# Batch attention in a perceiver kernel: norms inverted ahead of the rotation, spread in ScalarE's banks, and three moves with it

## The reference

```
q = l2norm(xn @ Wq); k = l2norm(xn @ Wk); v = xn @ Wv          # norm over the 32 features of a head
clock = softplus(xn @ clock_w + clock_b)                       # one value per token and head
q, k = rope(q), rope(k)
gcp = exp(clip(cumsum(-softplus(xn @ gate_w + gate_b)), -60, 50))
p_exp = exp(p - max(p)) * clock;  p_cs = cumsum(p_exp)         # p = xn @ p_w + p_b
q = q * gcp / (p_cs + 1e-8);  k = k / (gcp + 1e-8) * p_exp
out = softmax(causal(q k^T / sqrt(32))) @ v;  x1 = out @ out_w + out_b + residual
```

## Time and profile before

| what | value |
|---|---|
| time, median of 3 runs | 2138.5 us (2136.87 to 2139.09) |
| the profiled execution: its own time | 2137.74 us |
| its span | 2136.0 us |
| TensorE busy, granted clock over the span | 2058.3 us (96%), 0.988 |
| VectorE, ScalarE, GpSimd busy | 1230.1, 888.0, 60.9 us |

### The profile page before, as it was taken

One profiled execution on the slowest core, in us unless ns is written; L12 is line 12 of the kernel. 1 busy time (PEld: TensorE's weight loads), 2 busy tenths in 40 slices (PEclk: granted clock), 3 DMA queues, 4 the chain that ended last, 5 costly groups with the idle time before them and its releaser, 6 DMA issues. The chain is left out here.

```text
span 2136.0 us, 35519 instructions
## 1 busy us (share of the span) xinstructions
PE 2058.3 (96%) x14806; PEld 1499.0 (70%) x14806; DVE 1230.1 (58%) x2118; ACT 888.0 (42%) x2081; POOL 60.9 (3%) x78
## 2 busy tenths in 40 slices
PE   7999997999999999989999999999999999989999
PEld 6864454688868888744448887778778777775687
DVE  6446687653438888999996112443443534447563
ACT  4233532442333333689993332322322322333342
POOL 0000000000000000200000000000000000000122
PEclk9999998999999999999999999999999999999999
DMA  6300000112010111200021355211311311233001
GB/s 258 106 21 0 2 2 2 60 60 79 20 46 20 60 60 40 99 20 20 1 79 60 101 138 158 82 54 46 91 46 46 91 46 47 69 120 97 1 0 40
DMA packets 80223, 127.59 MB, mean 60 GB/s; under 512 B 7216, under 2 KB 40496, under 8 KB 79600
## 3 DMA queue, kind: packets, MB, share of 16 engines
q1 hardware_dynamic: 80064, 125.32, 18.5%
HBM read 110.23 MB, written 15.07 MB: 59 GB/s over the span
## 5 line engine op out<-in xcount | busy, mean ns | idle before, releaser
L1272 ACT ACTIVATE R<-bank 128x512 f32<-128x512 f32 (+3 forms) x151 | 89.2, 597 | 407.9 <-PE bank L945 325.5
L1538 ACT ACTIVATE R<-R 128x64 f32<-128x64 f32 x896 | 217.0, 342 | 3.3 <-DVE R L2241 3.3
L945 PE MATMUL bank<-cth,wmh 128*128 128x512 f32 x512 | 207.8, 406 | 9.3 <-ACT arena L1643 7.8
L945 PE MATMUL bank<-cth,wml 128*128 128x512 f32 x512 | 202.1, 395 | 0.0
L945 PE MATMUL bank<-ctl,wmh 128*128 128x512 f32 x512 | 201.9, 394 | 0.0
L522 PE MATMUL bank<-XN,arena 128*128 128x512 f32 x320 | 147.2, 612 | 0.0
L945 PEld LDWEIGHTS bank<-cth,wmh 128*128 128x128 f32 x512 | 96.1, 188 | 38.3 <-issue 17.3
L522 PE MATMUL bank<-Y,arena 128*128 128x512 f32 x256 | 115.9, 597 | 1.6 <-ACT H L1581 1.6
L2352 DVE COPY Y<-bank 128x512 f32<-128x512 f32 x128 | 79.2, 681 | 60.5 <-PE bank L994 60.5
L945 PEld LDWEIGHTS bank<-cth,wml 128*128 128x128 f32 x512 | 96.1, 188 | 22.3
L522 PEld LDWEIGHTS bank<-XN,arena 128*128 128x128 f32 x320 | 60.9, 196 | 71.1 <-issue 70.7
(11 more groups left out here) (432 smaller groups left out, 4311.2 us busy)
## 6 DMA issues: line engine op xcount, KB each, us to landing
H<-in_ctxT SPq DMA_DIRECT2D x30, 512.0 KB, 5.1
arena<-in_L_attn_mlp_w SPq DMA_DIRECT2D x8, 1024.0 KB, 5.3
R<-value_rows SPq DMA_DIRECT2D x32, 132.0 KB
arena<-in_L_ffn_Wg SPq DMA_DIRECT2D x4, 1024.0 KB, 6.9
arena<-in_L_ffn_Wu SPq DMA_DIRECT2D x4, 1024.0 KB, 5.2
arena<-in_L_ffn_Wd SPq DMA_DIRECT2D x4, 1024.0 KB, 5.6
arena<-in_downT SPq DMA_DIRECT2D x4, 1024.0 KB, 6.4
arena<-in_up_rows SPq DMA_DIRECT2D x4, 1024.0 KB, 6.7
```

The costliest lines, as they stand in the source:

```text
L945: last = mm(b[:, :].rearrange("p (a c) -> p a c", a=2), w_, c_[:, k, :, :], start=(k == 0 and n_ == 0), stop=(k == 3 and n_ == 2))
L1272: fn(dst, src, ACT.Copy).then_inc(act_bank_free, 1)
L1538: last = fn(into[:, x // 2, h, :, x % 2], RC["Ey"][:, t, h, :], ACT.Copy, scale=RC["Ex"][:, t, h, 8 * j + x:8 * j + x + 1])
```

## The change

Five edits that go together. On VectorE, `norm(o)` runs ahead of `rotate(o)`, and `spread_norm(o+1)` directly behind `rotate(o+1)`, with `normalise(o)` last in the pass. `norm_spread` opens its four units in ScalarE's banks instead of VectorE's; VectorE still reads them, waits on ScalarE's full count and counts them free in ScalarE's free count. To keep the counts in order, `norm_spread(o)` first waits for ScalarE's copy of ("bp", o+1, 1), for group 3 of ("bo1", 2, 1), and ScalarE waits for the last spread bank of group 3 before it copies ("bo1", 3, 1). `clocks(o+1)` moves from ahead of `scores(o)` to between its halves, and `gate_unit(o+2, 0)` from there to behind the scores.

```diff
--- before.py
+++ after.py
@@ -670,15 +670,16 @@
 
             def norm_spread(o):
                 pe.wait_ge(S["b_rn"], o + 1)
+                on_act(("bp", o + 1, 1) if o < 3 else ("bo1", 2, 1))
                 for c in range(C2):
-                    two = [open_dve(("n", o, i, c)) for i in range(2)]
+                    two = [open_act(("n", o, i, c)) for i in range(2)]
                     for s_ in range(4):
                         for i in range(2):
                             j = 32 * (2 * i + c)
                             last = mm(two[i][:, tl(s_)], tab("expand")[j:j + 32, tl(s_)], norms[j:j + 32, :], start=True, stop=True,
                                       tile_position=(j, 0))
                             if s_ == 3:
-                                last.then_inc(dve_bank_full, 1)
+                                last.then_inc(act_bank_full, 1)
 
             def gate_unit(o, c):
                 b = open_dve(("bg", o, c))
@@ -694,10 +695,10 @@
                            tab("causal")[hp, :].unsqueeze(1).to_broadcast([32, TT, 32]), start=True, stop=False,
                            tile_position=(32 * h, 32 * i), skip_group_check=True)
                 for tt in range(TT):
-                    if tt == 4 and o < 2:
-                        gate_unit(o + 2, 0)
+                    if tt == 4 and o < 3:
+                        clocks(o + 1)
                     if tt % 4 == 0:
-                        on_dve(("n", o, 1, tt // 4))
+                        on_act(("n", o, 1, tt // 4))
                     for i in range(4):
                         tok = slice(128 * tt + 32 * i, 128 * tt + 32 * i + 32)
                         for h in range(4):
@@ -766,10 +767,9 @@
             project(1, ("bp",))
             norm_spread(0)
             for o in range(4):
-                if o < 3:
-                    clocks(o + 1)
                 scores(o)
                 if o < 2:
+                    gate_unit(o + 2, 0)
                     gate_unit(o + 2, 1)
                 if o:
                     turn(o - 1)
@@ -1427,6 +1427,8 @@
 
             def first_sums(o, c):
                 act.wait_ge(S["b_cos"], 7)
+                if (o, c) == (3, 1):
+                    act.wait_ge(act_bank_free, UA.at[("n", 3, 1, 1)] + 1)
                 copy_out(first_out[o][:, ch(c)], unit(("bo1", o, c))[:, :])
 
             def turned(o):
@@ -2045,8 +2047,9 @@
             def spread_norm(o):
                 for c in range(C2):
                     for i, x in enumerate((q, k)):
-                        b = unit(("n", o, i, c))
-                        v.tensor_tensor(x[:, ch(c)], b[:, :], x[:, ch(c)], ALU.mult).then_inc(dve_bank_free, 1)
+                        u = UA.at[("n", o, i, c)]
+                        dve.wait_ge(act_bank_full, u + 1)
+                        v.tensor_tensor(x[:, ch(c)], UA.banks[u % 4][:, :], x[:, ch(c)], ALU.mult).then_inc(act_bank_free, 1)
 
             def normalise(o):
 
@@ -2064,17 +2067,16 @@
                 step(last)
 
             gates(0)
+            norm(0)
             rotate(0)
-            norm(0)
             spread_norm(0)
             for o in range(4):
                 if o < 3:
                     gates(o + 1)
+                    norm(o + 1)
                     rotate(o + 1)
-                    norm(o + 1)
+                    spread_norm(o + 1)
                 normalise(o)
-                if o < 3:
-                    spread_norm(o + 1)
                 if o == 2:
                     first_sums(1)
             first_sums(0)
```

## The result

The changed kernel takes 2156.82 us (median of 4 runs, 2154.55 to 2158.56) against 2137.68 us for the kernel before beside it: ratio 1.0094, 95% interval 1.0081 to 1.0107. The median is 19.1 us higher (the ratio that goes with the interval is not exactly the quotient of the medians); 15.1 us more and a median of 2153.6 us were forecast. The profiled execution took 2157.12 us, its span 2155.3 us against 2136.0.

The account below looks back on a forecast made before the run. TensorE, busy 96% of the span, was taken to set the pace. Waits and reordering gave 12.6 us, clock and issue 2.5, in all 15.1, so a median of 2153.6 us, own range 2148 to 2158, full range 2140 to 2165.

Parts of the forecast that it names:

- A: Start of the attention: norm_spread(0) waits for ScalarE's copy of ("bp", 1, 1), +1.4 us.
- B: Scores of groups 0 to 2: masks wait for the spread products and the clocks lose their cover, +5.1 us.
- C: Before values in groups 1 to 3: early inversion waits for roots, freeing the rotation bank 2.4 us later, +7.2 us.
- D: Before norm_spread: waits for normalise of 0.51 and 1.82 us go, smaller waits for ScalarE copies come, -1.1 us.
- F: Low clock and issue waits in attention: clocks +6.0, gate unit -1.9, issue -1.6, "bp" behind the standstill 0; +2.5 us.
- R1: Rival: the clock falls in values too, 20 to 29 us more, 2159 to 2168 us; chance 0.12.
- Group 3: Last group, without clocks: masks 6.70 us behind the spread, taken as unchanged, bounds -2 and +1 us.
- R3: Rival: VectorE is the bound and gets faster, showing at norm_spread, -5.6 us, 2133 us; chance 0.09.
- R4: Rival: effects cancel in the attention, time within 0.2%, 2138 us; chance 0.07.
- R2: Rival: small loss, low-clock stretch shortens and issue waits vanish, 4.3 to 9 us more, 2143 to 2147; chance 0.14.

Follow-up runs that it names:

- e4: Kernel before with only the clock factors moved between the halves of the scores and the first gate unit behind them; ratio 1.0003.
- e5: Kernel before with only the spread put in ScalarE's banks, clock factors still ahead of the scores; ratio 1.0006.
- e8: Kernel before with spread in ScalarE's banks and clock factors inside the scores together, normalise still ahead of the products; ratio 1.0037.
- e2: Kernel before with one edit, the norms inverted ahead of the rotation; 2142.0 us, ratio 1.0038.
- e11: Kernel before with norms inverted ahead of the rotation and TensorE's norm sums ahead of its rotations; ratio 1.0012.
- e10: The changed kernel measured again, nothing altered, against the kernel before; ratio 1.0086.
- e6: Kernel before with only group 3's spread in ScalarE's banks and its products ahead of normalise; ratio 0.9992.

## Why the prediction was right

**A, the start: right.** The wait of `norm_spread(0)` is 1.29 us, forecast 1.4 (it starts 1.6 us later). The profile calls it "issue"; ScalarE's copies end at 222.58 + 1.25 = 223.83, 0.10 us before the spread.

**B, the banks: right in size and in mechanism.** Masks stand 3.86 us behind the spread in all three passes (3.8 forecast), waiting 2.14 us each (1.5 to 2 forecast), and the clock factors came on top. The forecast said that their old place was the cover; e4, e5 and e8 show it: neither edit costs anything that can be told alone, both together 7.9 us. The Trainium skill's rule in "Perfetto Trace Analysis", section "Matmuls", that independent groups should rotate through different banks, is borne out by e8 (1.0037) but not by e5 (1.0006), where the same groups share a set with 2 us of other work between them. The forecast's words that the rows of before have no wait at the masks hold for groups 0 to 2; in group 3 shows 0.84 us for a ScalarE copy.

**C, the inversion ahead: right.** Three waits of 2.35 us, forecast 2.4, and VectorE's own of 2.15, 3.02 and 2.55 us before the clamp (7.7 in all). e2 shows that the edit makes these waits alone, e11 that it is the lateness of the roots, not the place in VectorE's stream.

**D: right.** `normalise` is no longer waited for; 0.79 us is left before the last spread (forecast 0.85). The forecast named two places in which TensorE waited for VectorE; the earlier trace rows shows a third, 0.31 us before the clock factors for the products, too small to matter.

**F, clock and issue: the mis-sized term.** Three parts came as taken or better: clock factors 4.00 + 3.78 + 3.78 us instead of three times 2.0, +5.6 (6.0 taken); gate units and projections behind them 22.66 and 8.10 us instead of 6.67 + 17.43 and 5.39 + 3.70, -2.4 (-1.9 taken); issue waits of groups 0 and 2 gone, -3.2 (-1.6 taken). But the part taken as 0, on the ground that the clock had held 1.00 in values, was 4.5 us: after the standstill the values and the first projection or partial sum ran slow. Projections took 5.40 and 4.32 us instead of 3.70, the partial sum 3.39 instead of 1.98, the values themselves 1.98 and 1.54 instead of 1.35. That is rival R1 at half its bound or less: the bound of 10.5 counts a projection half in each group, but in pass 2 a partial sum of 1.98 us stands there, so it should have been 9.0. The row of before had been measured without a standstill ahead of it and could not stand for the case with one. The Trainium skill, "TensorE: Matmul & The Clock Gate", section "What's actually happening", holds the slow clock to be the default that activity releases. The traces agree with it here: over the changed kernel, e10 and e2, eight of nine such standstills have a fall behind them, each worth 1.2 to 1.7 us, and in the ten traces without the standstill, the kernel before among them, the same places run at full speed, to 0.1 us. A further 1.0 us came in the projections of pass 2 (15.04 us instead of 14.02) and 0.6 in the second halves of the scores.

Group 3, taken as unchanged with a bound of -2, gave 1.9 back: its spread and first sums ran at full speed (1.72 and 1.98 us instead of 2.65 and 3.28 in the kernel before). Together: A 1.3, B 5.4, C 7.1, D -1.1, F 6.1, group 3 -1.9, in all 16.9; measured in the attention 16.6.

So A to D were forecast at 12.6 us and came to 12.7 for the reasons given, while the closeness of the whole is in part luck: F was 3.6 us too small, group 3 hid 1.9 of it, and the 2.7 us behind the attention are no part of the account. The profiled execution, 19.4 us above the one before, lies at the upper edge of the forecast's 10 to 20 us, next to R1.

R3 (VectorE as the bound) and R4 are refuted by the waits themselves and by the time. R2 had one thing right, the issue waits behind the clock factors.

## What to carry to other kernels

A wait costs what is left over after the work that stands in front of it, so an edit that adds a wait and one that moves the work in front of it must be priced as a pair: here each alone left the time where it was and both together cost 8 us. Where work is moved earlier on one engine, ask first whether its input is there earlier too; if not, everything behind it, and every buffer that it holds, comes later. And on TensorE a new standstill is to be priced with the slower matmuls behind it, here 7.1 us of waiting and 4.5 us of low clock; whether the whole stage loses that much depends on what low clock it saves or adds elsewhere.

## What the runs showed of the hardware that was not expected

The price of a standstill in clock is steady where it stands and varies over the stage. Behind the three standstills at the values the matmuls lost 4.5 us in the changed kernel, 4.3 in e2 and 3.3 in e10. Yet the granted clock of e2 between 222 and 426 us has a mean of 0.93, no lower than the 0.92 before:

```profile
222.00:426.00 204.00, 183.86 (x2801) 103.58 (x2800) 153.07 (x187) 75.99 (x117) 0.00 (x0) 0.93 0.05 17
```

In e2 other work ran faster than in the kernel before: the gate units in the scores of groups 0 and 1 took 5.14 and 3.70 us instead of 6.67 and 5.39, the first sums behind the last spread 1.98 instead of 3.28. With 2.2 us less waiting for `normalise` this is why e2's attention is only 3.2 us longer in its trace than the one before, for 7.1 us of waiting and 4.3 of low clock. In the changed kernel the gate units and projections saved 2.4 us and the group 3 part 1.9, but the clock factors lost 5.6 to the low clock of the scores. A mean over the stage hides this; the durations of the same instructions at the same place show it. What decides where else the low clock stands is not shown: kernels with the same order in a pass had it in different places (the gate unit of group 1 took 5.39 us before and 3.70 in e6).
